# Four conditioned layers on one core: the adapter's small jobs and three max jobs at other places in the schedule

## What is computed

```python
# layer 0: state-space mixing, conditioned by t, then an MLP
y_mod = _ln(y) * (1 + scale_a) + shift_a
y = y + gate_a * _s5(y_mod)
y_mod = (_ln(y) * (1 + scale_c) + shift_c) * (1 + scale_ff) + shift_ff
y = y + gate_ff * (gelu(y_mod @ W1 + b1) @ W2 + b2)
# layer 1: attention with one head of 256, then an MLP
# layer 2: the adapter; its weights are themselves computed from the condition
h = gelu(_layernorm(ada_emb, ln_g, ln_b) @ W1 + b1)
w = h @ W2 + b2                       # 4 maps of 256 x 8 for each sequence
y = x @ a1 @ bb1; y = gelu(y) @ a2 @ bb2 + x
# layer 3: attention with 16 heads of 16
att = softmax(einsum('bhqd,bhkd->bhqk', q, k)) / D ** 0.5
out = einsum('bhqk,bhkd->bhqd', att, v)
```

## Time and profile before

| | us |
|---|---|
| median of 3 timed runs | 879.87 (879.1 to 881.4) |
| the profiled execution | 880.76 |
| its span, first to last instruction | 878.9 |
| PE busy | 838.7 |
| DVE busy | 666.1 |
| ACT busy | 459.4 |
| POOL busy | 227.3 |

### The profile page before, as it was taken

The page is one execution under the profiler, slowest core; times in us unless marked ns, Lnnn a source line. Parts: engine busy times, 40 slices in busy tenths (PEclk is TensorE's granted clock), DMA queues, the critical chain, the costliest instruction groups (busy, mean ns, idle before and its releaser), DMA issues.

```text
span 878.9 us, 13287 instructions
## 1 busy us (share of the span) xinstructions
PE 838.7 (95%) x4978; PEld 521.8 (59%) x4978; DVE 666.1 (76%) x1139; ACT 459.4 (52%) x840; POOL 227.3 (26%) x377
## 2 busy tenths in 40 slices
PE   6999999999999999999989989999999999999994
PEld 3668888958977998887845433333333333333342
DVE  8998657676538577646458879999999999999377
ACT  4646232144332443333232158888878878888760
POOL 4443412202002103112112710233333333333411
PEclk9999999999999999999989969999999999999998
DMA  8613122110000000000597600505050505000002
GB/s 314 252 49 97 55 92 98 49 52 2 1 1 1 1 1 1 2 1 1 168 182 193 252 1 3 92 21 92 21 93 21 92 21 93 23 27 24 27 25 73
DMA packets 29379, 57.40 MB, mean 65 GB/s; under 512 B 7228, under 2 KB 15152, under 8 KB 29314
## 3 DMA queue, kind: packets, MB, share of 16 engines
q1 hardware_dynamic: 22596, 44.40, 19.2%
q0 software_dynamic: 6720, 12.15, 4.7%
HBM read 39.26 MB, written 14.91 MB: 62 GB/s over the span
## 4 chain that ended last, share of the span: by engine, by line
PE 83%; DVE 8%; ACT 5%; POOL 2%; issue 2%; DMA 0%; DVEq 0%; ACTq 0%; POOLq 0%
PE PA L1531 15%; PE PA L1542 15%; PE PD L1327 10%; PE PA L1305 8%; PE PA L1253 7%; PE PD L1502 7%; PE PA L1408 5%; PE PD L1378 4%; PE PA L1246 2%; PE PA L1398 1%; PE PD L1600 1%; DVE NMX L2045 1%; PE PA L1477 1%; ACT R L1107 1%; PE PD L1253 1%
## 5 line engine op out<-in xcount | busy, mean ns | idle before, releaser
L2045 DVE TENSOR_REDUCE NMX<-PD 128x2 f32<-128x1024 f32 x256 | 301.9, 1220 | 25.7 <-PE PD L1502 21.2
L1107 ACT ACTIVATE R<-PA 128x512 f32<-128x512 f32 x512 | 267.0, 603 | 71.6 <-PE PA L1531 69.8
L1531 PE MATMUL PA<-STKR 50*128 50x512 f32 x512 | 185.3, 454 | 3.6 <-ACT R L1107 2.5
L1531 PEld LDWEIGHTS PA<-STKR 50*128 50x128 f32 x512 | 83.2, 188 | 151.7 <-ACT R L1107 139.3
L1502 PE MATMUL PD<-STKR 48*128 48x512 f32 x512 | 150.0, 456 | 4.2 <-DVE NMX L2045 4.1
L1043 ACT ACTIVATE R<-PA,VEC 128x512 f32<-128x512 f32 x64 | 43.8, 687 | 104.1 <-PE PA L1305 91.6
L1327 PE MATMUL PD<-WHR,HSR 128*128 128x256 f32 x512 | 95.3, 285 | 0.5 <-DVE HSR L1918 0.5
L1327 PEld LDWEIGHTS PD<-WHR,HSR 128*128 128x128 f32 x512 | 82.1, 191 | 6.1 <-issue 2.0
L1305 PE MATMUL PA<-XSR,WHR 128*128 128x512 f32 x256 | 81.2, 398 | 3.9 <-issue 2.0
L1502 PEld LDWEIGHTS PD<-STKR 48*128 48x128 f32 x512 | 62.0, 188 | 30.1 <-DVE NMX L2045 13.4
L1327 PE MATMUL PD<-WLR,HSR 128*128 128x256 f32 x256 | 72.4, 283 | 0.0
(11 more groups left out here) (288 smaller groups left out, 1181.3 us busy)
## 6 DMA issues: line engine op xcount, KB each, us to landing
STKR<-qk_terms SPq DMA_DIRECT2D x32, 384.0 KB, 8.8
R<-in_l_w SPq DMA_DIRECT2D x8, 1024.0 KB, 5.0
W<-in_w SPq DMA_DIRECT2D x4, 1024.0 KB, 10.7
qk_terms<-PARTS SPq DMA_DIRECT2D x8, 512.0 KB, 3.4
qk_terms<-PARTS POOLq DMA_DIRECT2D x8, 512.0 KB, 3.8
S<-row_reciprocals POOLq DMA_DIRECT2D x56, 64.0 KB, 2.1
X<-in_x SPq DMA_DIRECT2D x4, 512.0 KB, 8.5
qk_terms<-PARTS SPq DMA_DIRECT2D x8, 256.0 KB, 5.0
```

The lines of the kernel that those rows point to most:

```text
L1107: act.activation(PB[:, n % 2, j, :], PA[:, e % NEB, :], ACT.Exp).then_inc(s_exp3, 1)
L1531: pe.matmul(PA[:, e % NEB, :], KS[rows, slot(gg), jj, kt * P:(kt + 1) * P], QS[rows, slot(gg), jj, c * HALF:(c + 1) * HALF], start=True, s ...
L2045: ve.tensor_reduce(out, PD[:, o:o + NROW, :], axis=AX_X, op=ALU.max, negate=True).then_inc(s_mred, 1)
```

## The change

Only the list is edited; every engine does the same instructions on the same data. In the opening, `ad` 0 goes from ahead of `gc` 0 to behind `y0` 0, `ad` 1 behind `bu` 2, `ad` 2 from behind `bu` 2 to behind `ya` 1, and `lr` 0 from behind `gk` 1 to behind `y0` 1. `lr` 1, 2 and 3 move from behind `ya` 1, from ahead of `d0` 0 and from behind `d0` 3 to ahead of `d0` 0, behind `d0` 1 and behind `d0` 4. In the second place, a second max job follows behind every other Q/K job (three times), so that three lone max jobs instead of six end the row, and `tm` 0 stands behind max job 17 between Q/K jobs 13 and 14, no longer behind the last Q/K job.

```diff
-         ("an", 0), ("nn", 1), ("ya", 0), ("n0", 1), ("ad", 0), ("gc", 0), ("cg", 1), ("y0", 0), ("yn", 0), ("ad", 1), ("bu", 2),
-         ("ad", 2), ("ws", 0), ("bu", 3), ("yn", 1), ("gk", 1), ("lr", 0), ("bg", 0), ("ma", 0), ("ya", 1), ("lr", 1),
-         ("y0", 1), ("mb", 0)]
-FIRST = mlps(0, "m", {0: [None, ("ws", 1), ("yn", 2), ("yn", 3), None, ("lr", 2)], 4: [("lr", 3)], 6: [("gb", 0)],
+         ("an", 0), ("nn", 1), ("ya", 0), ("n0", 1), ("gc", 0), ("cg", 1), ("y0", 0), ("ad", 0), ("yn", 0), ("bu", 2), ("ad", 1),
+         ("ws", 0), ("bu", 3), ("yn", 1), ("gk", 1), ("bg", 0), ("ma", 0), ("ya", 1), ("ad", 2), ("y0", 1), ("lr", 0), ("mb", 0)]
+FIRST = mlps(0, "m", {0: [None, ("ws", 1), ("yn", 2), ("yn", 3), None, ("lr", 1)], 2: [("lr", 2)], 5: [("lr", 3)], 6: [("gb", 0)],
...
-SCHED += weave([("qk3", QJOBS + j) for j in range(QJOBS - 1)], [("mx", EARLY + j) for j in range(QJOBS - 1)])
-EARLY += QJOBS - 1
-assert UNIT == EARLY
-SCHED += [("qk3", 2 * QJOBS - 1), ("mx", EARLY), ("tm", 0)]
-SCHED += weave([("v3", TWO + j) for j in range(TWO)], [("mx", EARLY + 1 + j) for j in range(TWO)])
-SCHED += [("mx", n) for n in range(EARLY + 1 + TWO, LEAD)]
+for j in range(QJOBS):
+    SCHED += [("qk3", QJOBS + j), ("mx", EARLY)]
+    EARLY += 1
+    if j % 2 and j < QJOBS - 1:
+        SCHED.append(("mx", EARLY))
+        EARLY += 1
+    if UNIT < EARLY <= UNIT + 2 and ("tm", 0) not in SCHED:
+        SCHED.append(("tm", 0))
+SCHED += weave([("v3", TWO + j) for j in range(TWO)], [("mx", EARLY + j) for j in range(TWO)])
+SCHED += [("mx", n) for n in range(EARLY + TWO, LEAD)]
```

## The result

The changed kernel took **885.0 us** (median of eight runs, 882.1 to 886.0), the kernel before 880.46 in the runs beside it; the ratio is 1.0045, with an interval from 1.0028 to 1.0062. The forecast was 881.3 with a range up to 883.4: the sign is right, the size is short by 3.7 us. By the prediction's own bound (over 882.5 is slower) the change is slower, which had been given 0.20.

A forecast was written before the change was run, and what follows sets the result against it. The prediction took PE to bound the kernel, busy 838.7 of 878.9 us, with DVE and ACT close to its path. Opening +2.0 and max jobs -0.5 gave +1.5 on 879.87, so 881.3 us, range 877.7 to 883.4.

The forecast's parts named there:

- the prediction's own bound: Whole kernel: a measurement tells apart 2.64 us; under 877.2 is faster, over 882.5 slower (chance 0.20).
- What bounds the kernel, and the opening's chain: PE bounds, busy 838.7 of 878.9 us; opening waits become 1.6 at ad1, 1.3 at y0 of sequence 1, 0.7 at lr0.
- DVE's wait for WHR: Opening: DVE waits 2.3 us for the high half of the first MLP weight, queued behind ACT's Gelu.
- The opening's sum: Opening: 1.6 + 1.3 + 0.7 - 1.49 = 2.1 late, taken as +2.0, between +0.8 and +3.1.
- The chain through ACT: Opening: late Gelu delays the weight's halves and DVE by 1.3; rival that it does not bind: 876.4, chance 0.09.
- The max part: Ahead of the last attention: waits of 3.2 become 1.2, tm0 waits 1.9; taken as -0.5, bounds -2.2 and +0.3.
- with the clock behind it as before: First attention steps: the half clock behind the max jobs was assumed unchanged within the -0.5 for the max part.
- the rival on the kept clock: First attention steps: PE keeps 2.4 GHz, saving 3.4 us, total 877.9; chance 0.17.
- The slower rival: At tm0 among the Q/K jobs: the clock falls at the new wait, 1.9 us more, total 883.2; chance 0.16.
- The base: Whole kernel: the forecast was applied to 879.87 us, the median of three timed runs.
- The sum: Whole kernel: +2.0 for the opening and -0.5 for the max jobs give +1.5, forecast 881.3 us.

The follow-up runs named there:

- e1_open: The kernel before with only the opening part of the change, max jobs as before: 884.05 us, ratio 1.0034.
- e5: The changed kernel with tm0 moved back behind the last Q/K job: 880.29 us, ratio 1.0002.
- e6: The kernel before with unread products in PE's waits among the lone max jobs and behind the first energies: 876.73 us, ratio 0.9962.
- e7: The changed kernel with unread products ahead of its last lone max job (two) and behind the first energies (three): 880.72 us, ratio 0.9995.
- e9: The kernel before with the max part, tm0 kept late, and unread products ahead of the last lone max job and behind the first energies: 876.31 us, ratio 0.9929.
- e11: The kernel before with three unread products behind the first energies only: 879.73 us, ratio 0.9972.
- e16: The changed kernel with three unread products behind the first energies only: 879.63 us, ratio 0.9986.
- e10: The kernel before with five unread products in the waits of its lone max jobs only: 882.28 us, ratio 0.9990.
- e13_in_steps: The changed kernel with one unread product of 128 rows in each of attention steps 1, 2 and 3: 885.32 us, ratio 1.0058.

## Why the prediction was wrong, point by point

*What bounds the kernel, and the opening's chain* held. PE's waits at y0 and lr0 came with the releasers that were named (POOL, DVE). The one at ad1 is shown as "issue", not as DVE, but DVE's copy ended 0.10 ahead of ad1 (52.27 + 0.13 and 52.50), so the chain is the one named. I had 1.6, 1.3 and 0.7; the trace has 1.33, 1.41 and 0.43, and 0.49 at the first half of y0, where I had said "to speak of" none. Together with the 1.49 removed that is 2.17, and I had 2.1; the nearness is partly luck, since e1_open has the same cost with no 0.49 and a sum of 1.58. The first down product is 1.07 late, forecast 1.1. DVE's wait for WHR is 2.34, forecast 2.3, and WLR took 2.29, as taken.

*The opening's sum failed by 0.45.* It was counted as 2.1 and taken as +2.0, with lr2 at 1.0. The job takes 1.07 on PE, and the products behind it start later by 1.19 than without it; and 0.2 more is lost in small waits of the two layers that follow, where I had expected 0.2 to be won. The value is 2.46, inside the bounds of 0.8 and 3.1.

*The chain through ACT* was the right mechanism for part of it: taking it away gave 0.98. The rest I put to the order of PE's own queue (ad1 behind bu2, needing a copy that stands behind statistics; and lr2 behind the first down product instead of ahead of it). No version here removed it, so that is argued from the rows.

*The max part.* "I take -0.5 for the part": it gave 0.49 up to the energies, in both kernels with tm0 early, 0.15 by fewer waits and 0.26 by the clock ahead of the energies, where I had -0.1 to -0.3 and 0.2. With no wait at tm0 it is 2.1, and the bound given was 2.2.

**The step that failed is "with the clock behind it as before".** I had two cases for the clock, kept or as before, and priced a kept one at 3.4 (3.1 to 3.2 measured). I did not consider the third: that the clock lasts through the lone max jobs and falls inside the steps. There PE has hardly a wait left for the half clock to run under, so in the max part alone the same 13.7 us cost 1.44 more in the steps; and in the full change the stretch was longer too, 17.1 us, and cost 2.8 in both profiles. Against the filled versions, which have no stretch, the steps lose 5.9 us to 17.1 at half clock in the changed kernel, and 3.1 to 13.7 in the kernel before. So the rival on the kept clock had the right place, and what speaks for it (three of the four short waits go) was true and not enough. The wait behind the energies, which I had listed against it, decides in the changed kernel: filled, the clock is kept. Why the stretch is longer there is not shown. The changed kernel and e5 differ only in tm0's place, 12 to 16 us ahead of the energies, and have 17.1 and 6.8 us. The Trainium skill (TensorE: Matmul & The Clock Gate, Part 1) says that activity releases the throttle. The trace does not agree in this stretch: from 519 to 529 PE was busy for 10.00 of 10.00 us and the granted clock stayed at 0.50.

*The slower rival* (a fall at tm0) was given 0.16 and 1.9 us. It is not in the two profiles of the full change, but it came in one of the six profiles that have this wait, with 1.7. Without the fall the wait at tm0 costs 1.6, which the sum had.

*The base.* The forecast was put on 879.87, the median of three runs; all 116 runs of the kernel before in these comparisons have 880.8. That is 0.9 us.

*The sum.* 880.8 + 2.46 - 0.49 = 882.8 without a word on the clock, against 883.7 over all eighteen runs and 885.0 in the first eight. With the clock of its profile it would be 882.8 + 2.8 = 885.6, where the slowest runs are. So of the 3.7 us by which the first median missed, 0.9 is the base and 0.45 the opening. The rest, 2.2 to 2.3, I put to the clock, and over all eighteen runs it is only 0.9. This part is shown by profiles alone. The timed runs give only the sum of the time at half clock, and that is not longer in the changed kernel: 28.0 us on average over its eighteen runs and 29.4 over the 116 of the kernel before, worked out from each run's span and mean clock. By the profiles it is the place of the stretch that costs, and no run without a profile tells where it lay.

*What stays open.* What sets the length of a stretch at half clock: the groups of the table hold together, but no theory here forecasts them all (the fall of the versions with tm0 late comes inside the steps too and lasts 6.8 us, against 13.7 and 17.1). PE's wait at ad1, the first cause in the opening, could by the rows be taken off by another order of DVE's statistics, which was not tried. Nor was it tried whether narrower products fill a wait as well.

## What to carry to other kernels

Price an idle stretch of PE not by its length alone but by the clock behind it: products that nobody reads, in 1.6 to 4.8 us of waits, gave 2.5 to 4.4 us in five versions (e6, e7, e9, e11, e16). In a sixth (e10) they filled 3.2 us and gave 0.9, which is inside the noise, because the clock fell behind the one wait left empty. And a change that took most of those waits away and left the last one moved the fall to a worse place. The place of a stretch at half clock counts as much as its length: over PE's waits it is cheap, over a row without waits it is dear. When a job is moved next to another that shares its pair of banks, look at the reduction that frees the bank: a transpose of 0.27 us cost 1.6 only by standing one place too near. A small job of a feeding engine (a Gelu of two rows) is to be moved together with what is queued behind it.

## What the runs showed of the hardware

- The granted clock stayed at 0.50 for 17.1 us (515.5 to 532.6 in the changed kernel) while PE was busy almost throughout, and came back after 6.8 us in a version with the same fall and wide products among the steps, one of them inside the stretch (e13_in_steps, one profile).
- It fell with no single wait of PE longer than 1.94 us in the row ahead: at 512.4 behind waits of 0.28 and 1.80, and at 493.8 at the end of one of 1.94.
- A straight line through all 288 runs of all kernels (span against time at half clock, worked out from each run's span and mean granted clock, with an offset for each kernel) gives 0.36 us for each us at half clock, and leaves 0.7 us of scatter. In the steps the rows give the same: 1 - 2.60 / 4.07 = 0.36.
- The wait for the first weight at the kernel's start was between 1.0 and 2.9 us in these profiles, and the product behind it started between 9.3 and 10.9 us, a spread of more than half of what was to be measured.
